# Cross-attention and feed-forward block: four of a chunk's sixteen row-maximum steps at other beats

## The reference

```
x = x + tanh(g_xattn) * attention(layernorm(x), context)     # 16 heads of 32, softmax over 154 keys
x = x + tanh(g_ffn) * ffn(layernorm(x))                      # 512 -> 2048 -> 512
ffn: h = relu(x @ w1.T + b1); out = round8(h) @ round8(w2).T + round16(b2); out = round16(out)
```

## Time and profile before

| What | us |
|---|---|
| median of 3 runs | 1660.89 (1660.31 to 1663.74) |
| the profiled execution | 1664.15 |
| its span | 1662.4 |
| PE busy | 1538.4 (93%) |
| DVE busy | 941.5 (57%) |
| POOL busy | 864.2 (52%) |
| ACT busy | 812.9 (49%) |
| PE waiting for a row maximum (line 555 for line 919) | 42.5 in all |

### The profile page before, as it was taken

One profiled execution on the slowest core, in us unless ns is written; L12 is line 12 of the kernel. 1 busy time (PEld: TensorE's weight loads), 2 busy tenths in 40 slices (PEclk: granted clock), 3 DMA queues, 4 the chain that ended last, 5 costly groups with the idle time before them and its releaser, 6 DMA issues.

```text
span 1662.4 us, 23615 instructions
## 1 busy us (share of the span) xinstructions
PE 1538.4 (93%) x8552; PEld 695.3 (42%) x8552; DVE 941.5 (57%) x1303; ACT 812.9 (49%) x1187; POOL 864.2 (52%) x916
## 2 busy tenths in 40 slices
PE   5765599999989999999989999999989999999998
PEld 3321244444434444444434444444434444444443
DVE  6667546465565656566565746556564655646231
ACT  2355465454535555454625545464535545553511
POOL 1465547364464746465465746465464646545320
PEclk8986899999999999999999999999999999999999
DMA  7243444344442434344352443343343444332110
GB/s 277 61 137 80 112 137 110 112 98 114 77 125 77 114 103 99 108 105 118 72 133 73 105 124 93 104 109 101 90 101 109 99 108 102 90 96 78 48 51 26
DMA packets 249879, 169.30 MB, mean 102 GB/s; under 512 B 165484, under 2 KB 214948, under 8 KB 248100
## 3 DMA queue, kind: packets, MB, share of 16 engines
q1 hardware_dynamic: 247124, 162.08, 37.3%
q10 hardware_dynamic: 2640, 5.72, 0.9%
HBM read 73.36 MB, written 33.55 MB: 64 GB/s over the span
## 4 chain that ended last, share of the span: by engine, by line
PE 56%; DVE 13%; SPq 13%; POOL 6%; issue 5%; DMA 4%; ACT 2%; ACTq 1%; DVEq 0%
PE ring L471 34%; PE ring L643 13%; SPq L354 5%; SPq L331 3%; DVE y L941 3%; PE m_ps L555 2%; DMA resid<-in_x 2%; DVE smax L919 2%; PE s_ps L582 2%; SPq L363 2%; DVE xn L990 2%; DVE resid L981 2%; POOL resid L1086 2%; DVE bns L964 2%; POOL pmain L1054 2%
## 5 line engine op out<-in xcount | busy, mean ns | idle before, releaser
L471 PE MATMUL ring<-late_a,w 128*128 128x512 f16 x3072 | 698.7, 380 | 7.6 <-DMA late_a<-x 7.6
L471 PEld LDWEIGHTS ring<-late_a,w 128*128 128x128 f16 x3072 | 297.8, 98 | 359.7 <-issue 23.8
L1054 POOL TENSOR_TENSOR pmain<-p,pmain 128x512 f16<-128x512 f32 x256 | 304.6, 1192 | 143.2 <-ACT p L727 141.5
L748 ACT ACTIVATE late_b<-ring,b_sb,wsc 128x512 fp8e4<-128x512 f32 x256 | 199.3, 779 | 335.3 <-PE ring L471 335.3
L919 DVE TENSOR_REDUCE smax<-m_ps 128x4 f32<-128x616 f32 x256 | 202.8, 792 | 193.9 <-PE m_ps L555 193.6
L941 DVE RECIPROCAL y<-d_ps 128x256 f32<-128x256 f32 x128 | 224.0, 1750 | 90.6 <-PE d_ps L601 90.6
L727 ACT ACTIVATE p<-s_ps,prob_log,sc 128x512 f32<-128x512 f32 x320 | 247.7, 774 | 0.0
L643 PE MATMUL ring<-w,late_b 128*128 128x512 fp8e4 x1024 | 229.6, 380 | 1.4 <-ACT late_b L748 0.9
L1054 POOL TENSOR_TENSOR pleft<-p,pleft 128x512 f16<-128x512 f32 x64 | 75.1, 1173 | 245.9 <-ACT p L727 245.9
L724 ACT ACTIVATE pmain<-s_ps,prob_log,sc 128x512 f16<-128x512 f32 x256 | 198.0, 774 | 0.9 <-PE s_ps L582 0.9
L471 PE MATMUL ring<-wo,yT 128*128 128x512 f16 x768 | 177.9, 382 | 0.0
(11 more groups left out here) (144 smaller groups left out, 1418.4 us busy)
## 6 DMA issues: line engine op xcount, KB each, us to landing
qstack<-qparts SPq DMA_DIRECT2D x384, 64.0 KB, 2.1
pstack<-left_rows SPq DMA_DIRECT2D x192, 128.0 KB, 2.6
xin<-in_x SPq DMA_DIRECT2D x64, 256.0 KB, 3.2
left_rows<-pleft SPq DMA_DIRECT2D x64, 256.0 KB, 3.1
resid<-in_x SPq DMA_DIRECT2D x64, 256.0 KB, 3.1
out_x<-resid SPq DMA_DIRECT2D x64, 256.0 KB, 2.7
resid<-in_w_t SPq DMA_DIRECT2D x4, 1024.0 KB, 5.2
qstack<-negT SPq DMA_DIRECT2D x128, 2.0 KB, 1.7
```

Source lines behind the costliest of these rows:

```text
L471: last = pe.matmul(dst, lhs(a, k), rhs(b, k), start=(k == 0 and p == 0), stop=(k == n_k - 1 and p == 2))
L748: nc.scalar.activation(hT[:, j, :], ring_bank("h", c, j)[:], ACT.Relu, bias=b1_sb[:, j:j + 1], scale=wsc[:, j // 4, 1:2], saturate=False). ...
L1054: nc.gpsimd.tensor_tensor(part[:, 1, :], p32[:, n % 2, :], part[:, 0, :], ALU.subtract).then_inc(prob_lo, 1)
```

## The change

```diff
-MAX_AT = [-10, -9, -8, -7, -6, -5, -4, -3, 2, 3, 4, 5, 6, 7, 8, 9]
-SHIFT_AT = [-3, 9]
+MAX_AT = [-10, -9, -8, -7, -6, -5, -4, -3, -2, -1, 2, 3, 4, 5, 10, 11]
+SHIFT_AT = [-3, 11]
...
-KBLK_AT = [-18]
+KBLK_AT = [-15]
```

## The result

| kernel | median us (range, runs) | ratio to before, 95% interval |
|---|---|---|
| before | 1661.13 (1660.29 to 1663.74, 6) | 1 |
| changed | 1667.74 (1665.89 to 1669.27, 6) | 1.0038 (1.0025 to 1.0051) |
| before, measured with the later experiments | 1662.28 (1658.65 to 1664.55, 25) | 1 |
| changed, measured again beside it | 1666.10 (1664.89 to 1669.59, 9) | 1.0027 (1.0017 to 1.0037) |

The first two rows belong together, and so do the last two. The change makes the kernel slower, by 6.6 us in the first comparison and 3.8 us in the second (0.38 and 0.27% by the ratios, whose intervals leave out 1). The forecast was 3.6 us slower.

A forecast was written before the change was run, and what follows sets the result against it. PE's list was taken to set the time. Chunk terms of 6.1 + 0.3 - 2.9 - 1.5 = +2.0 us plus +1.6 for the clock gave +3.6 on 1660.9: 1664.5 us, range 1655 to 1673.

The forecast's parts named there:

- Beats 6 to 9: Four ranks leave, the 1.35 us wait at beat 9 goes, and the fourth ln2_apply comes 1.58 us earlier.
- The wait at beat 11: Rank of beat 11 waits 1.96 us (about 1.8 as recorded) for beat 10's maximum, behind fourth ln2_apply and first finish.
- A steady chunk: +0.09 us from the moved wait plus 0.52 for ranks at beats -2 and -1: +0.61 each, ten chunks +6.1.
- Chunk 1: PE's wait for the last transposed tile ends earlier: -2.9 us, or only -1.6 if SP keeps both transposes behind POOL.
- Chunk 2: DVE's chain sets the end; third ffn_out at 286.59 against 288.13: -1.5 us.
- TensorE's clock: Waits near 2 us may drop the clock to 1.2 GHz; one drop taken of 0 to 13: +1.6 us.
- chunks 4, 8, 12: First chunks of a batch: the 0.52 us vanishes in the pstack wait, the chain gives +0.09 each: +0.3 us.
- Collision gone: Rival: fourth ln2_apply meets no POOL operation, beat 10's maximum 0.83 us earlier in 14 chunks; 1651 us, chance 0.13.
- half collision: Rival: second ln2_apply runs free, third collides less; about -3.6 us, 1659 us with one clock drop; chance 0.13.
- No wait at beat 11: Rival: the change works fully, beat 10's maximum released 2 us earlier than the chain gives; 1637 us, chance 0.05.
- It doesn't do what it says: Rival: something other than the maxima holds DVE at beats 5 to 9; near 1661 to 1664 us, chance 0.08.
- Clock falls in most chunks: Rival: 10 or more clock drops of 1.6 us, 1679 to 1684 us; falls often, chance 0.11.

The follow-up runs named there:

- the run with kblk's load alone: The kernel before with only KBLK_AT changed, -18 to -15, so kblk's four DMAs issue behind kcat's 12; measured 1662.68 us, ratio 1.0007.

## Why the prediction was right

The two medians give +6.6 and +3.8 us for a forecast of +3.6. Behind the number, the mechanism was right where it mattered: the wait leaves beat 9 and stands at beat 11, behind the fourth ln2_apply and the first finish. Some of the parts came out other than counted, and twice the errors cancelled by luck.

**Beats 6 to 9.** Confirmed in place; the size came out by small errors that cancel. Counted from the maximum of beat 5, the fourth ln2_apply came at +18.39 (1044.87 - 1026.48), against +19.96 before (the 665.84 of the earlier trace rows less that maximum's start at 645.88, a row not shown): 1.57 us earlier, where 1.58 was forecast. But the steps differ. Without the maximum of beat 6 the first ln2_apply started 0.20 earlier, about as forecast, but it took 1.48 instead of 1.31, so next to nothing was left (0.02 to 0.03). Those of beats 7 and 8 gave 0.70 each. The second ln2_apply took 0.56 instead of 0.98, which gave 0.42, and the third 0.81 instead of 0.54, which took 0.27 back: a POOL operation had begun 0.6 us before it:

```profile
1040.61 1.15 POOL L1054 TENSOR_TENSOR pmain<-p,pmain 128x512 f16<-128x512 f32 x1
```

**The wait at beat 11.** Confirmed: 1.84 as recorded, forecast about 1.8. The rank came 22.63 us after that of beat 5 (1048.65 - 1026.02), forecast 22.60 (668.02 - 645.42). It was not the same everywhere: over 2 us in three chunks of the first profile (6, 9 and 12) and in two of the second (12 and 13), and 1.25 to 1.41 in chunks 8 and 15.

**A steady chunk.** Forecast +0.61. In the second profile of the changed kernel this rank stands at 953.32, 1046.86 and 1140.41, a period of 93.54; before, the rank of beat 9 stood 92.90 and 92.95 us apart in chunks 5 to 7. So +0.6 in these. Single chunks scatter, since the wait before was not always 1.2 us (0.68 in chunk 12, 1.73 in 14 and 0.52 in 15 of the first profile; the prediction's "within 0.2 us" leaves these out), but over all ten the mean is +0.64.

**Chunk 1.** Forecast -2.9. In the second profile of the changed kernel and the first of the kernel before, PE's ranks of chunk 1 from 119.09 to 143.8 us stand within 0.01 us of each other, so the two can be laid side by side from there. These are hidden of chunk 1, the rank of beat -2 of chunk 2 and its late rank in the changed kernel:

```profile
193.73 4.52 PE L471 MATMUL ring<-late_a,w 128*128 128x512 f16 x12 [3.12 <-issue]
...
238.30 0.42 PE L555 MATMUL m_ps<-kblk,qparts 128*128 128x308 f16 x2 [1.18 <-DVE smax L919]
...
283.22 0.42 PE L555 MATMUL m_ps<-kblk,qparts 128*128 128x308 f16 x2 [1.84 <-DVE smax L919]
```

193.73 against 196.76 is -3.0.

**Chunk 2.** Forecast -1.5. The third ffn_out follows at 283.22 + 0.26 = 283.48, against 288.13; that is -4.65, of which -3.03 were chunk 1's, leaving -1.6. The number is right by luck, the reasoning was not. These are the rank of beat 5 and its maximum in chunk 2, in the changed kernel and then in the kernel before:

```profile
260.59 0.43 PE L555 MATMUL m_ps<-kblk,qparts 128*128 128x308 f16 x2
261.05 0.80 DVE L919 TENSOR_REDUCE smax<-m_ps 128x4 f32<-128x616 f32 x1 [1.24 <-PE m_ps L555]
```

```profile
261.72 0.43 PE L555 MATMUL m_ps<-kblk,qparts 128*128 128x308 f16 x2
262.18 0.80 DVE L919 TENSOR_REDUCE smax<-m_ps 128x4 f32<-128x616 f32 x1 [1.24 <-PE m_ps L555]
```

Of the 3.03 us won in chunk 1 only 1.13 are left here. The ranks of beats -2 and -1 cost 0.52 us, and the one at 238.30 waits, which was forecast not to happen (1.18 us, 1.35 start to start). DVE stands 1.24 us for PE at beat 5, so what PE lost before that is passed on: 1.9 us that the prediction had at nothing. Against it, from the rank of beat 5 to the third ffn_out the changed kernel takes 22.9 us, about as in a steady chunk, and the kernel before 26.4. It had two more waits for a maximum there (0.64 and 0.28 us), one of 2.08 and the drop of TensorE's clock, and its fourth ln2_apply came 22.0 us behind the maximum of beat 5 and not 20.0. So the chain became 3.6 us shorter, not 1.58. That stretch is not always so long. In the run with kblk's load alone, neither the wait of 0.64 us nor the drop was there:

```profile
278.77 0.42 PE L555 MATMUL m_ps<-kblk,qparts 128*128 128x308 f16 x2 [2.07 <-DVE smax L919]
279.04 3.61 PE L643 MATMUL ring<-w,late_b 128*128 128x512 fp8e4 x16
```

There the third ffn_out started 23.7 us behind the maximum of beat 5 (286.38 - 262.64), against 26.0 in the first profile of the kernel before and 22.4 in the changed kernel.

In chunk 1 the ranks of beats -2 and -1 wait as well, 3.76 and 0.98 us, but DVE's list is no later there by beat 6 (its first ln1_apply starts at 173.79, before at 173.81). In the steady chunks they do not wait.

**TensorE's clock.** Forecast one drop of 1.6 us; one and two were seen, of 1.7 each. The choice of one was a guess between the ends, and it was at the low side. The drop of the kernel before in chunk 2 went away at the same time; it is part of the 1.6 us of that chunk.

**The sum.** For the second profile of the changed kernel and the first of the kernel before, read at the third ffn_out of chunks 2 and 15 (283.48 and 1525.07 against 288.13 and 1519.64):

| term | forecast | measured |
|---|---|---|
| chunk 1 | -2.9 | -3.0 |
| chunk 2 | -1.5 | -1.6 |
| ten steady chunks | +6.1 | +6.4 |
| chunks 4, 8, 12 | +0.3 | +0.3 |
| clock | +1.6 | +3.4 |
| together | +3.6 | +5.4 |

The terms are rounded. The spans differ by 1667.8 - 1662.4 = 5.4 us as well. With the one drop of the first profile the terms give about +3.7, and its span is 1666.0, 3.6 us more. Against the second profile of the kernel before (1660.8) the same two differences are 7.0 and 5.2: 1.6 us lie between two profiles of one kernel. The rows carry the sign and most of the size. The first comparison of medians lies 3 us above the forecast; drops and varying waits are of that size, but executions without a profile don't show which it was.

**The rivals.** *Collision gone*: it was not; the fourth ln2_apply took 1.37 again, with POOL's operation 0.07 us ahead of it. Of the half collision, the second ln2_apply did run free, but the third collided more and not less. *No wait at beat 11*: out in this kernel, and its price is about right once the maxima are one beat later (forecast 24 us below the kernel before, measured 20). *It doesn't do what it says*: out, beat 9 is clear. *Clock falls in most chunks*: out.

## What to carry to other kernels

When an instruction that others wait for is moved in an engine's list, look at what stands directly ahead of it at its new place, and when that is due, not at how full the engine is: here one beat decided between some 5 us more and 20 us less than before. What was freed by moving the instruction was worth nothing, because the next meeting of the two engines came before the slower one had caught up. For the steady chunks this could be read from one chunk, by following both lists from one meeting point to the next. The chunks at the start have to be followed by themselves, and a difference that comes out right there says little: in chunk 2 two errors of 1.9 and 2.0 us cancelled.

## What the runs showed of the hardware

In the two profiles of the changed kernel the granted clock fell behind three waits of 2.05 us or so, never behind those of 1.7 to 1.9, and it also stayed up behind others of that length:

```profile
1242.76 0.42 PE L555 MATMUL m_ps<-kblk,qparts 128*128 128x308 f16 x2 [2.06 <-DVE smax L919]
1243.02 7.07 PE L643 MATMUL ring<-w,late_b 128*128 128x512 fp8e4 x32
```

So the length of the wait alone doesn't decide it. What PE did just before goes with it. In all three falls the second ffn_out had come late too: it started 4.21 to 4.35 us behind the first one, against 3.94 and 3.98 in the two chunks of that length without a fall (12 and 6 of the first profile). In chunk 2 of the kernel before, the two profiles with a fall have an idle time of 0.64 or 0.47 us at beat 6 and one of 0.28 at beat 7 ahead of the 2.08; the run with kblk's load alone has only the 0.28 ahead of its 2.07, and no fall. Among the eight waits of 2.05 to 2.08 us these are five falls and three without, told apart by some tenths of a us of further idle time. Two waits of 1.99 and 2.01 (chunks 8 and 4 of the first profile of the kernel before) had no fall either. This is what the rows have in common; no run varied it on purpose.

A partly overlapped POOL operation cost DVE according to its head start. For ln2_apply (0.54 us undisturbed) beside a POOL operation of 1.15 us, the rows of steady chunks give 1.37 us with a head start of 0.07, 0.98 with 0.45, 0.82 with 0.62 and 0.56 with 0.88.
